# Setting up the first two batches of an attention and mixture-of-experts kernel in another order

## The reference, cut to what matters

```python
# x, ctx: (16, 256, 256); 16 heads of 16; D = 256
def _L0_xattn_ref(Q, K, V, mask, Wq_w, Wq_b, Wk_w, Wk_b, Wv_w, Wv_b, Wo_w, Wo_b):
    q = (Q @ Wq_w + Wq_b).reshape(b, tq, H, DK).transpose(0, 2, 1, 3)
    k = (K @ Wk_w + Wk_b).reshape(b, tk, H, DK).transpose(0, 2, 1, 3)
    v = (V @ Wv_w + Wv_b).reshape(b, tk, H, DK).transpose(0, 2, 1, 3)
    scores = jnp.einsum('bhqd,bhkd->bhqk', q, k) / jnp.sqrt(jnp.float32(DK))
    scores = jnp.where(mask == 0, jnp.float32(-1000000000.0), scores)
    attn = jax.nn.softmax(scores, axis=-1)
    out = jnp.einsum('bhqk,bhkd->bhqd', attn, v)
    return out.transpose(0, 2, 1, 3).reshape(b, tq, c) @ Wo_w + Wo_b

x = x + _L0_xattn_ref(_layernorm(x), ctx, ctx, mask, ...)
x = x + _L0_ffn_ref(_layernorm(x), ...)   # 8 experts, top 2, and a shared expert
```

## Time and profile before

| | us |
|---|---|
| median of three runs | 790.56 |
| lowest and highest | 788.26, 790.91 |
| the profiled execution | 788.83 |
| its span in the profile | 787.0 |
| TensorE busy in it | 736.9 |

### The profile page before, as it was taken

One profiled execution on the slowest core, in us unless ns is written; L12 is line 12 of the kernel. 1 busy time (PEld: TensorE's weight loads), 2 busy tenths in 40 slices (PEclk: granted clock), 3 DMA queues, 4 the chain that ended last, 5 costly groups with the idle time before them and its releaser, 6 DMA issues.

```text
span 787.0 us, 22011 instructions
## 1 busy us (share of the span) xinstructions
PE 736.9 (94%) x8171; PEld 463.6 (59%) x8171; DVE 534.4 (68%) x1142; ACT 396.1 (50%) x679; POOL 348.3 (44%) x520
## 2 busy tenths in 40 slices
PE   4789999999999999998989889899999999998998
PEld 3545555555556565554456446677777777755655
DVE  6766688888988989887656777433333333358897
ACT  4225566666666666766644553344444444433331
POOL 6152134466665555566575260111122111267774
PEclk9879999999999999999999999999999999999999
DMA  6744555555554455557341232798899989634743
GB/s 181 190 141 145 180 162 161 140 152 173 155 163 151 149 151 141 160 160 207 98 143 55 81 136 54 155 155 179 159 169 172 163 172 164 151 114 128 240 149 114
DMA packets 164234, 118.26 MB, mean 150 GB/s; under 512 B 108450, under 2 KB 143522, under 8 KB 164132
## 3 DMA queue, kind: packets, MB, share of 16 engines
q1 hardware_dynamic: 145844, 79.65, 42.4%
q0 software_dynamic: 10272, 28.88, 12.2%
q10 hardware_dynamic: 8016, 8.33, 3.3%
HBM read 52.78 MB, written 38.14 MB: 116 GB/s over the span
## 4 chain that ended last, share of the span: by engine, by line
PE 63%; DVE 17%; DMA 6%; issue 5%; ACT 4%; POOL 2%; SPq 2%; DVEq 0%; ACTq 0%; POOLq 0%
PE ps_st L1924 16%; PE ps_m L1939 9%; PE ps_st L1495 7%; PE ps_st L1133 6%; DVE mx L1023 5%; PE ps_o L1184 5%; PE ps_m L1207 4%; PE ps_st L1152 2%; PE ps_o L1506 2%; DMA qk_scratch<-arena 2%; PE ps_m L1343 2%; PE ps_st L1168 2%; PE ps_m L1506 2%; PE ps_m L1283 2%; ACT p L826 1%
## 5 line engine op out<-in xcount | busy, mean ns | idle before, releaser
L1023 DVE TENSOR_REDUCE mx<-ps_st 128x4 f32<-128x1024 f32 x128 | 155.6, 1217 | 31.0 <-PE ps_st L1152 23.8
L826 ACT ACTIVATE p<-ps_st 128x1024 f32<-128x1024 f32 x128 | 131.0, 1024 | 76.3 <-PE ps_st L1168 73.5
L1924 PE MATMUL ps_st<-fwh,p 128*128 x568 | 137.9, 313 | 2.3 <-DMA p<-expert_rows 2.3
L1696 POOL DMA_DIRECT2D sorted_out<-p x71 | 38.4, 541 | 181.7 <-ACT p L1753 178.1
L1427 POOL DMA_INDIRECT expert_rows<-hrow,slot x64 | 64.8, 1012 | 75.3 <-DVE slot L1418 55.2
L1924 PE MATMUL ps_st<-fwl,p 128*128 x284 | 88.8, 313 | 0.0
L1924 PEld LDWEIGHTS ps_st<-fwh,p 128*128 128x128 f16 x568 | 55.4, 98 | 29.6 <-issue 3.1
L1133 PE MATMUL ps_st<-maskq,identb 64*64 64x512 bf16 x512 | 52.8, 403 | 15.9 <-DVE mx L1023 13.0
L1495 PE MATMUL ps_st<-q,arena 128*128 128x512 f16 x264 | 59.7, 380 | 4.6 <-DVE qk L1806 2.5
L1495 PE MATMUL ps_st<-qk,arena 128*128 128x512 f16 x264 | 61.2, 387 | 1.7 <-DVE qk L941 1.6
L1753 ACT ACTIVATE p<-ps_m 128x256 f32<-128x256 f32 x71 | 27.3, 384 | 70.3 <-PE ps_m L1939 68.2
(11 more groups left out here) (235 smaller groups left out, 1769.1 us busy)
## 6 DMA issues: line engine op xcount, KB each, us to landing
sorted_out<-p POOLq DMA_DIRECT2D x71, 128.0 KB, 3.0
qk_scratch<-arena SPq DMA_DIRECT2D x32, 256.0 KB, 2.6
arena<-ffn_dram SPq DMA_DIRECT2D x15, 544.0 KB
qk<-qk_scratch SPq DMA_DIRECT2D x44, 128.0 KB, 3.0
arena<-ctx_dram SPq DMA_DIRECT2D x16, 256.0 KB
hT_dram<-hT ACTq DMA_DIRECT2D x16, 256.0 KB, 2.3
out_dram<-xr SPq DMA_DIRECT2D x16, 256.0 KB, 3.3
xr<-x_dram SPq DMA_DIRECT2D x7, 512.0 KB, 4.2
```

The costliest lines, as they stand in the source:

```text
L826: eng.activation(expo[n % 4][:, :, :], ps_st[pair["T", n]][:, :].rearrange("p (h q) -> p h q", h=4), ACT.Exp, scale=SCALE).then_inc(s_e, 1)
L1023: eng.tensor_reduce(mx[b % 2][:, qt, :].rearrange("p (h g j) -> p h g j", h=2, g=HG)[:, :, hg, :], ps_st[pair["S", 8 * b + n]][:, :].rearr ...
L1696: eng.dma_start(sorted_out[k * P:(k + 1) * P, :], ys[k % 3][:, :]).then_inc(r_st[k % 3], 16)
L1924: last = mm(o[:, 0:INTER], xgT[k % NXG][:, xl, dc, :], (fwh, fwl)[wl][:, bass.ds(e, 1), w0 + dc * INTER:w0 + (dc + 1) * INTER], start=dc = ...
```

## The change

- VectorE, not GpSimd, sets `ks[0]` and `vx[0]` to ones, behind its own clearing of `bhl` and ahead of `stats(0)` (semaphore `s_set`). GpSimd sets `ks[1]`, `vx[1]`, `vx[2]` first of all and `ks[2]` last, behind the low half of the output weights.
- The four transposes of the mask go from unit 2, ahead of q of batch 0, to unit 4, behind v of batch 0, and write to `ps_st[0]` in place of a bank of the ring, which so has one use less. ACT copies them to `mb_k` there.
- v of batch 0 goes from unit 5, behind xt of batch 1, to unit 4, right behind k of batch 0.
- `nrm` of batch 1 goes from unit 4 to unit 5, so that on VectorE the low half of k of batch 0 stands ahead of it.
- SP issues the two copies for `turned_k` behind the reads of q and k of batch 0, not ahead of the load of the output weights; each pair of mask copies has a semaphore of its own.

```diff
-        s_turn = sem("s_turn")
+        s_turnq = sem("s_turnq"); s_turnk = sem("s_turnk"); s_set = sem("s_set")
...
-        when.update({("stats", 1): 3, ("nrm", 1): 4, ("xt", 1): 5, ("ct", 1): 6, ("q", 1): 7, ("k", 1): 7, ("v", 1): 10,
+        when.update({("v", 0): 4, ("stats", 1): 3, ("nrm", 1): 5, ("xt", 1): 5, ("ct", 1): 6, ("q", 1): 7, ("k", 1): 7, ("v", 1): 10,
...
-                if (i, u) == (0, 2):
-                    order += ["mask"]
...
+        mask_to = ps_st[0][:, 0:TT * SEQ]
...
-            for s_mask, plain, turned in ((s_mbk, mb_k, turned_k), (s_mbq, mb_q, turned_q)):
-                eng.wait_ge(s_mask, 1)
+            def turn_mask(plain, turned, s_out):
                 for c in range(2):
-                    eng.dma_start(turned[64 - 64 * c:128 - 64 * c, :, :], plain[64 * c:64 * c + 64, :, :]).then_inc(s_turn, 16)
+                    eng.dma_start(turned[64 - 64 * c:128 - 64 * c, :, :], plain[64 * c:64 * c + 64, :, :]).then_inc(s_out, 16)
+
+            eng.wait_ge(s_mbq, 1)
+            turn_mask(mb_q, turned_q, s_turnq)
...
-                    if i == 0:
-                        eng.wait_ge(s_const, 7)
+                    if i < 3:
+                        eng.wait_ge(*((s_set, 1), (s_const, 2), (s_const, 5))[i])
...
+                if i == 0:
+                    eng.wait_ge(s_mbk, 1)
+                    turn_mask(mb_k, turned_k, s_turnk)
...
-            for i in range(2):
-                eng.memset(ks[i][:, :, :], 1.0).then_inc(s_const, 1)
-                eng.memset(vx[i][:, :, :, :], 1.0).then_inc(s_const, 1)
+            eng.memset(ks[1][:, :, :], 1.0).then_inc(s_const, 1)
+            eng.memset(vx[1][:, :, :, :], 1.0).then_inc(s_const, 1)
+            eng.memset(vx[2][:, :, :, :], 1.0).then_inc(s_const, 1)
...
             power(1)
-            eng.memset(ks[2][:, :, :], 1.0).then_inc(s_const, 1)
-            eng.memset(vx[2][:, :, :, :], 1.0).then_inc(s_const, 1)
-            eng.wait_ge(s_const, 7)
...
+            eng.memset(ks[2][:, :, :], 1.0).then_inc(s_const, 1)
...
             eng.memset(bhl[:, :], 0.0).then_inc(s_ones, 1)
+            eng.memset(ks[0][:, :, :], 1.0).then_inc(s_set, 1)
+            eng.memset(vx[0][:, :, :, :], 1.0).then_inc(s_set, 1)
             stats(0)
...
-                    if (i, u) == (0, 2):
-                        wait_bank(eng, "mask")
+                    if (i, u) == (0, 4):
                         eng.wait_ge(s_mbf, 1)
...
-                                last = eng.transpose(bank("mask")[:, at:at + P], nz[:, qt, kt * P:(kt + 1) * P], ident[:, :])
+                                last = eng.transpose(mask_to[:, at:at + P], nz[:, qt, kt * P:(kt + 1) * P], ident[:, :])
```

More of the change, by code:

```diff
@@ L738, in values_out @@
                 eng.wait_ge(s_v, b + 1)
-                if b == 0:
-                    eng.wait_ge(s_const, 7)
+                if b < 3:
+                    eng.wait_ge(*((s_set, 2), (s_const, 3), (s_const, 4))[b])
                 if b >= 3:
@@ L809, in _ @@
                         eng.activation(bhl[0:1, :], b32[0:1, :], ACT.Copy).then_inc(s_bh, 1)
-                        eng.wait_ge(s_mbT, 1)
-                        eng.activation(mb_k[:, :, :], bank("mask")[:, :].rearrange("p (t q) -> p t q", t=TT),
-                                       ACT.Copy).then_inc(s_mbk, 1)
-                        eng.wait_ge(s_mbk, 1)
-                        eng.nop().then_inc(free("mask"), 1)
                         eng.wait_ge(s_id, 16)
@@ L817, in _ @@
                         eng.activation(identh[:, :], ident[:, :], ACT.Copy).then_inc(s_idb, 1)
+                    if (i, u) == (0, 4):
+                        eng.wait_ge(s_mbT, 1)
+                        eng.activation(mb_k[:, :, :], mask_to.rearrange("p (t q) -> p t q", t=TT), ACT.Copy).then_inc(s_mbk, 1)
                     _, st, pv = units(i, u)
@@ L1143, in scores @@
                     eng.wait_ge(s_idb, 1)
-                    eng.wait_ge(s_turn, 64)
+                    eng.wait_ge(s_turnq, 32)
+                    eng.wait_ge(s_mbk, 1)
                 wait_pair(eng, ("S", 8 * b + n))
@@ L1160, in scores_t @@
                     eng.wait_ge(s_mr[b % 3], 32 * (b // 3 + 1))
+                if b == 0 and n == 0:
+                    eng.wait_ge(s_turnk, 32)
                 wait_pair(eng, ("T", 8 * b + n))
```

## The result

The changed kernel is slower. Its median is 795.37 us against 791.52 of the kernel before, a ratio of 1.0056 with a 95% interval from 1.0035 to 1.0077; the forecast was 787.6 us, a gain of 2 us. Run three times more, each time beside the kernel before, it gave 1.0020, 1.0012 and 1.0031. So four occasions put the loss between 1 and 4.5 us, and it varies with the occasion more than one interval says; the experiments tell a part of why. Both kernels' runs spread over some 7 to 12 us, and a few per mille need many of them.

A forecast was written before the change was run, and what follows sets the result against it. TensorE is nearly always busy from 120 us, so the change lies in its gaps in the first 30 us: first `mx` from 28.46 to 26.5, 2.0 us gained, from 789.6 to 787.6 us; range 785.4 to 790.4.

The forecast's parts named there:

- part 1: Buffer 0's constants on VectorE: first statistics 0.4 us late, q and k of batch 0 +0.05, bounds -0.15 and +0.65.
- parts 2 and 4: Mask transposes off the ring: 0 gain; v of batch 0 follows k at 16.8, ends 18.4, with the mask 19.0.
- part 3: Keys' low half ahead of `nrm` of batch 1: ends at 18.0 against 20.01; scores could start at 25.1, -1.95 us.
- chain B: TensorE's own order up to the first scores: xt, ct, q and k of batch 1; expected to decide, by 0.6 us.
- part 5: `nrm` of batch 1 starts at 18.1 beside GpSimd's output weights and memset; ends 19.1 to 20.5, middle 19.8.
- X: Time at which `nrm` of batch 1 ends on VectorE, taken as 19.8 us.
- the sum: First `mx` from 28.46 to 26.5: 2.0 us gained, bounds 2.6 and 1.2, 0.6 less with memsets at their worst.
- the collision decides: Rival: xn also waits for `wol` and the `ks[2]` memset; gain 0.8 us or less; chance 0.25 including nothing handed on.
- part 6: xt, its copies, then q to the first `mx`: X + 6.7 = 26.5 against 28.46, -1.95 us.
- "slower" rival: TensorE waits longer, clock falls between 25 and 60 us: +3.5 us, 791.1, with the collision 792.3; chance 0.10.
- Handed on to the end: Assumption that what the first row maxima gain, from the first 30 us, reaches the end whole: 2 us.
- The claim that `nrm`'s end stays as it was and v's move carries the gain: Rival case: `nrm` still ends at 19.3; without v's move the first `mx` at X + 9.1; inside the forecast's 0.45.

The follow-up runs named there:

- both runs that fed it in the same wait: Changed kernel with the mask's four transposes made five times over, in TensorE's wait for the normalised rows: ratios 0.9998 and 0.9991 to the kernel before.
- `nrm` in unit 4: Changed kernel with `nrm` of batch 1 restored to unit 4, ahead of the keys' low half; three runs: ratios 0.9973, 0.9984 and 0.9972 to the kernel before.
- 56 products: Kernel before with 56 more mask products ahead of the very first scores, a delay with TensorE busy: ratio 1.0023 (1.0000 to 1.0045).
- 24 products: Kernel before with 24 more mask products ahead of the very first scores: ratio 0.9997 (0.9978 to 1.0016).
- memsets last: Kernel before with GpSimd's two memsets of the third buffers moved behind the output weights' subtraction: ratio 1.0027 (1.0003 to 1.0052).
- `nrm` in unit 4 with GpSimd's constants: Changed kernel with `nrm` of batch 1 back in unit 4 and all constants set by GpSimd: ratio 0.9988 (0.9967 to 1.0008).

## Why the prediction was wrong, point by point

- *Constants on VectorE* (part 1): right. The two memsets took 1.76 and 0.51 us and ended at 4.1 (I had 3.9), any started at 6.50, q's bias product at 12.81. Alone they are worth nothing that shows (28.59 against 28.46).
- *Mask out of the ring, values behind keys* (parts 2 and 4): right. v began at 16.80, right behind k, and ended at 18.5; the mask's transposes took 0.60.
- *Keys before `nrm`* (part 3): the low half ended at 17.96 as worked out, but the 7.0 us from there to the scores, which I held for a constant, were not one. Made as early in the kernel before, it moved the scores by 0.1 us (8.9 us from its end to them): SP's reads wait for the write of q, which stands behind other loads. I had read the row of the last event and not asked what else its queue waited for. In the changed kernel chain B decided. Where `nrm` stood in unit 4, though, the scores waited for the keys' load, 1.0 to 2.1 us, and started at 25.7 to 26.7, not at 25.1.
- *`nrm` against GpSimd* (part 5): this is the step that failed. I had the shortest X at 19.1 and the longest at 20.6, by the idea that the two VectorE instructions each wait out one GpSimd instruction. The first alone waited out all that was left of two, because the memset stood behind the subtraction without a wait between them; X was 21.5, 1.7 us past the 19.8 of the sum. The rival "the collision decides" named this mechanism and X = 21, and priced it at a gain of 0.8 or less.
- *Chain B from X* (part 6): X + 6.7 would have been 28.2, hardly a change to before. It was X + 9.6. Of the missing 2.9 us 2.5 are the clock: TensorE had waited 2.60 us and did most of the 28 products at half clock, and both runs that fed it in the same wait had X + 7.1. The sum had put nothing for it. Neither the forecast nor this rival put the clock on top of the wait; the "slower" rival had it only for the stage behind 25 us.
- *Handed on to the end*: a plain delay was still whole at the milestone in one execution; up to the end the profiles don't show it. The half-clock time behind 30 us, which the rivals priced at half a us for each us at most, cost some 0.7 in the table, up to 7 us in one execution.
- The base of the sum was low: I started from 789.6 us, and over thirteen runs the kernel before had a median of 791.52. With the right base the forecast of a gain would have missed all the same.
- The claim that `nrm`'s end stays as it was and v's move carries the gain: the first half was wrong (21.5, not 19.3). The second fits the three runs with `nrm` in unit 4, but no run has v's move alone.

## What to carry to other kernels

Before a VectorE instruction like this one (fp32, from SBUF to SBUF) is moved, lay GpSimd's queue beside its new start: count all that GpSimd will run there without a semaphore wait between, and price the VectorE instruction as lasting until the end of it, the worse of the two outcomes seen here. A wait of TensorE is to be priced with what follows it at half clock, here as much again. And where a chain goes through a DMA queue, moving its last input only helps if the queue's head isn't waiting for an earlier one.

## What the runs showed of the hardware

- A VectorE pair of 0.74 us took 3.27, 2.73, 2.17, 1.54 and 1.10 us where GpSimd was running; its longest instruction ended just behind GpSimd's running one and those queued behind that without a semaphore wait. With GpSimd idle it took 0.74. The Trainium skill (SBUF — State Buffer, section "Who interferes with whom") says that the one that comes first gets the shared port pair for its whole instruction; the rows agree, and add that a subtraction and a memset back to back left no opening between them (2954 ns through both).
- Two GpSimd instructions back to back don't always shut VectorE out, and GpSimd loses where it comes second. In five profiles VectorE's conversion of the mask (128x512, 0.43 us alone) came at 4.54 to 4.74 us, while one GpSimd memset ran until 4.93 and the next, of 544 elements, stood directly behind. In the kernel before and in that with 56 products VectorE got in between, was done at 5.20 and 5.21, and the second memset took 0.83 us instead of 0.55. In the other three (24 products, memsets last, `nrm` in unit 4 with GpSimd's constants) it waited for both, until 5.70; in the last of these a third memset stood behind and took 0.83 in its turn. The times of arrival don't tell the two outcomes apart, and no run shows what decides.
- A GpSimd memset, which reads nothing, held VectorE as the subtractions did (2.17 us for the pair of 0.74).
- VectorE's memset of 2048 fp16 elements took 1.76 us and that of 544 fp32 ones 0.51, so it goes by elements: 0.86 and 0.94 ns each.
- Products of 64 by 64 of the mask went through at 57 ns each when 60 stood in a row (3.43 us), where the first four of a unit take 0.41 us.
